# Small operations moved off VectorE in a six-layer decoder kernel: chains to GpSimd, mask and sums to TensorE, and a new walk

## The chip, the core and the metric

One core of a Trainium2 chip. The metric is the device time of one execution in microseconds, the median of several. The core has TensorE (PE, matrix products, its weight loads shown as PEld), VectorE (DVE), ScalarE (ACT), GpSimd (POOL) and SyncE (SP, which issues the DMAs). Each engine runs its own queue of instructions in order; they meet through semaphores.

## The reference

The input is x of 32 sequences, 128 tokens, 128 features, all float32, and a context of the same shape. Six blocks follow, and after each one `x = layernorm(x + block(x))`, without gain:

```
# L0_attn: a memory M (128x128) per sequence, two chunks of 64 tokens
y  = chunk @ M^T ; h = silu(y W1^T) W2^T + y                  # output of the chunk
km = mean(chunk / |chunk|) ; err = mean(h) - M km
M' = gate*(alpha*M + eta*err km^T) + (1-gate)*M ; M' *= min(30/(|M'|+1e-6), 1)
# L0_xattn: causal attention + x, norm (gain, bias), attention on the context + h, norm, relu(h W1 + b1) + h, norm, relu
# L0_ffn:   8 routed experts (4 with multipliers and a capacity) and a shared one
# L1_attn:  q,k,v = silu(conv4(x W)); T = I + tril(K K^T beta, -1) for chunks of 32; u = T^-1 v; w = T^-1 k; recurrence over
#           4 chunks; four causal filters of v (3, 7, 15, 31 taps); a router mixes the five paths; rms norm per head; Wo
# L1_xattn: attention on the context with biases
# L1_ffn:   top 2 of 4 experts; the third has two norms inside
```

## The kernel before

**Tiles.** The 32 sequences are 8 groups (`g` = 0 to 7) of 4 sequences, so that most tiles are 128 partitions by 512 elements (4 sequences of 128), of which one fills one of the 8 PSUM banks. Groups 0 to 3 and 6, 7 are loaded at the start; 6 and 7 run through the first two blocks early and are parked in DRAM; 4 and 5 are loaded when groups 0 and 1 leave. Each group runs through some 110 named steps; the first letter is the block (`a`, `x` with `c`, `f`, `b`, `y`, `g`).

**The order** of all steps is one text, `ORDER` (L38), written out by hand or by a planner that is not part of the kernel. `walk` reads it. Each engine's function (`sync`, `tensor`, `vector`, `scalar`, `gpsimd`) goes through the whole walk and issues what it has to do for a step. So the position in `ORDER` sets the place in every queue. `bank_table` deals out PSUM banks along the walk, each held until the step that `BANKS` names as the last.

**Steps that matter here.**

- *Norms.* `stats` on DVE (L1067) takes bn_stats and bn_aggr of each sequence, then makes the negated mean and the variance plus epsilon by two small instructions. POOL's `root` (L2101) takes the power -0.5 and multiplies the mean by it. ACT's `apply` (L1781) then normalizes in four instructions. There are 11 such norms per group (`STATS`), 88 in all.
- *The memory update.* DVE sums squares (`a_y`), makes silu from a tanh that ACT made (`a_s0`, `a_s1`), spreads the mean key (`a_km`), and makes the update's scalars by a chain of dependent instructions on 128x4 tiles (`a_dots` L1206, `a_c` L1239); POOL takes one square root in the chain.
- *Causal attention.* DVE adds the mask to the scores (`x_sc`, L1279), takes the row maximum and scales it; ACT makes the exponentials; DVE scales the product by the inverse sums and adds the residual (`x_pv`). In the attention on the context (`c_`), DVE multiplies the exponentials by the inverse sums (L1308) and TensorE adds the residual by a transposing product (`opened`, L492).
- *L1_attn.* TensorE makes the key norms and gates (`b_ss`, L790: eight products with 8 or 4 columns moving) and the query norms (`b_qn`, L803: four). DVE solves the triangular system by columns (`b_x`, 31 steps of two instructions, one multiplying and one subtracting).
- *L1_ffn.* `g_b0` (L961) makes the third expert's first product, `g_lg` (L966) the router's logits, four products each from the same input; DVE makes the weights (`g_wd`, L1691) and scales a transposed tile twice (`g_b2`, L1710). In L0_ffn, DVE splits the shares in three bfloat16 parts (`f_gl`, L1440).

`o.settle()` makes an engine wait for its own last linked instruction, so each dependent pair on one engine costs a semaphore's round.

Of the kernel before, what the change touches and what calls it, by code (L numbers as in the profile page):

```python
# [38 lines left out]
a_load/0 a_load/1 a_load/2 a_load/3 a_load/6 a_load/7 s_a a_y/0 a_s0/0 a_y/1 a_s0/1 c_v/0 a_ga/0 a_ga/1 c_v/1 a_km/0  # L39
a_km/1 a_err/0 a_err/1 a_dots/0 a_y/2 a_dots/1 a_c/0 a_y/3 a_s0/2 a_ga/2 s_x a_s1/0 a_c/1 c_v/2 a_km/2 a_out/0 a_s1/1  # L40
c_v/3 a_s0/3 s_f a_na/0 s_b1 s_b2 a_ga/3 x_tr/0 a_err/2 x_q/0 a_out/1 a_y/6 a_na/1 a_km/3 c_v/6 x_sc/0 a_dots/2 a_s0/6
x_ex/0 a_err/3 a_c/2 a_ga/6 x_tr/1 x_q/1 a_s1/2 c_v/7 a_dots/3 x_pT/0 x_sc/1 x_v/0 a_out/2 x_ex/1 a_km/6 x_pv/0 a_na/2
x_v/1 x_pT/1 a_y/7 x_tr/2 x_na/0 x_pv/1 x_q/2 a_s0/7 x_hF/0 x_v/2 c_q/0 s_y a_c/3 x_na/1 a_err/6 a_ga/7 a_s1/3 x_hF/1
a_km/7 c_sc/0 x_sc/2 c_ex/0 a_out/3 x_ex/2 c_q/1 a_dots/6 c_pT/0 a_err/7 c_pv/0 x_pT/2 a_na/3 a_c/6 c_sc/1 c_na/0
a_dots/7 x_pv/2 x_tr/3 c_hF/0 x_q/3 c_w1/0 a_s1/6 x_sc/3 c_ex/1 x_na/2 c_ft/0 s_g1 a_out/6 x_ex/3 x_v/3 c_fa/0 c_pT/1
x_hF/2 x_pT/3 s_g2 a_na/6 c_pv/1 c_nb/0 c_q/2 x_tr/6 s_g3 a_c/7 f_tr/0 c_na/1 x_pv/3 c_sc/2 a_s1/7 x_q/6 f_lg/0 x_na/3
f_mu/0 c_hF/1 f_hid.0-1/0 c_ex/2 a_out/7 x_v/6 c_w1/1 f_cnt/0 f_gl/0 x_hF/3 f_hid.2-4/0 c_ft/1 c_q/3 c_pT/2 a_na/7
x_sc/6 c_sc/3 f_gw/0 x_tr/7 f_hid.5/0 f_e.0-4/0 x_ex/6 c_fa/1 c_pv/2 x_q/7 f_e.5/0 c_ex/3 f_d.0-2/0 x_pT/6 x_sc/7
x_pv/6 c_nb/1 f_d.3-4/0 c_na/2 x_ex/7 f_d.5/0 c_pT/3 x_v/7 f_tr/1 x_na/6 f_out/0 f_na/0 c_pv/3 c_hF/2 c_na/3 x_pT/7
f_lg/1 f_mu/1 x_hF/6 c_w1/2 b_tr/0 c_hF/3 c_q/6 b_q/0 b_v/0 b_qs/0 b_q2/0 f_cnt/1 c_sc/6 f_hid.0/1 b_qn/0 b_vs/0  # L50
b_sh/0 b_k/0 b_vT/0 c_ft/2 b_ks/0 b_k2/0 f_hid.1-2/1 b_ez/0 x_pv/7 b_ss/0 c_ex/6 c_fa/2 f_hid.3-5/1 x_na/7 f_gl/1
c_w1/3 c_pT/6 b_fir.0-1/0 x_hF/7 c_nb/2 c_pv/6 c_q/7 f_gw/1 f_tr/2 c_sc/7 f_e.0-2/1 c_na/6 c_ft/3 c_ex/7 f_e.3-4/1
f_d.0/1 c_hF/6 f_e.5/1 f_d.1/1 c_w1/6 f_d.2/1 b_gg/0 f_d.3-4/1 c_ft/6 c_fa/3 c_fa/6 c_nb/3 c_nb/6 c_pT/7 c_park/6
f_d.5/1 f_out/1 f_na/1 b_fir.2-3/0 c_pv/7 c_na/7 b_tr/1 f_lg/2 f_mu/2 f_hid.0/2 b_v/1 b_q/1 b_kk/0 b_ag/0 b_sol/0
b_vs/1 b_sh/1 b_k/1 c_hF/7 b_qs/1 f_cnt/2 f_gl/2 b_q2/1 b_ks/1 b_k2/1 b_x.0-2/0 c_w1/7 f_hid.1/2 f_tr/3 b_x.3/0
f_hid.2/2 b_qn/1 b_x.4/0 f_gw/2 c_ft/7 b_x.5-9/0 f_hid.3-4/2 b_ez/1 f_e.0/2 b_x.10-11/0 c_fa/7 c_nb/7 f_e.1-2/2
c_park/7 b_vT/1 b_x.12-17/0 f_hid.5/2 b_fir.0/1 f_lg/3 b_ss/1 b_fir.1/1 f_d.0-2/2 f_e.3/2 f_mu/3 f_e.4/2 b_fir.2/1
f_hid.0-1/3 f_cnt/3 b_x.18/0 f_d.3/2 f_e.5/2 f_d.4-5/2 f_gl/3 f_out/2 f_hid.2-3/3 b_x.19/0 f_gw/3 f_hid.4/3
# [2224 lines left out]
```

## Time and profile before

| | us |
|---|---|
| three runs | 1147.06, 1147.66 (median), 1148.03 |
| the profiled execution | 1141.68 |
| its span, from first to last instruction | 1139.7 |
| PE busy | 1044.7 (92%) |
| DVE busy | 854.5 (75%) |
| ACT busy | 630.5 (55%) |
| POOL busy | 211.4 (19%) |

The profile's page lists busy time, the span in 40 slices, the DMA queues, the chain of work that ended last, and groups of instructions. The clock column is the TensorE clock that was granted, as a share of full speed. Busy time of PE is modelled, since products overlap in it.

### The profile page before, as it was taken

To read this page: it belongs to the slowest core of one execution; us is meant where nothing else is said; L and a number is where in the kernel's file an instruction comes from. 1 tells how busy PE (TensorE), PEld (TensorE's weight loads), DVE (VectorE), ACT (ScalarE), POOL (GpSimd) and SP (SyncE) were. 2 spreads that over 40 slices of the span, in tenths; PEclk is the share of its full clock that TensorE was granted. 3 is DMA by queue.
4 is the path that set the end of the run, shared out by engine and by line. 5 is a ranking of instruction groups with operands and counts; after the bars stand their busy time and mean duration, and the time that the engine had idled before them with its cause. 6 is when DMAs were issued, how large, how long until landed. Compare 5 with 4: busy or idle time off the path is not lost.

```text
span 1139.7 us, 21963 instructions
## 1 busy us (share of the span) xinstructions
PE 1044.7 (92%) x8036; PEld 714.2 (63%) x8036; DVE 854.5 (75%) x3375; ACT 630.5 (55%) x1341; POOL 211.4 (19%) x255
## 2 busy tenths in 40 slices
PE   5988889979998899999999967999998899999996
PEld 4767565545555577577777844464555567676775
DVE  3889998888869775777776468885988856787544
ACT  2466788674562124567777654645553134688662
POOL 0222223312121010222121120003131011331100
PEclk9899999988997589999999977999988699999998
DMA  9200001030243110001010000012242110000000
GB/s 336 89 1 1 1 1 47 10 74 11 56 91 69 20 30 2 18 2 38 2 28 10 18 20 10 1 46 57 68 93 56 38 29 10 10 11 1 1 10 28
DMA packets 71643, 41.24 MB, mean 36 GB/s; under 512 B 52208, under 2 KB 63856, under 8 KB 71280
## 3 DMA queue, kind: packets, MB, share of 16 engines
q1 hardware_dynamic: 71536, 39.84, 13.3%
q8 instruction: 64, 1.05, 0.4%
q14 instruction: 43, 0.35, 0.1%
HBM read 30.92 MB, written 8.91 MB: 35 GB/s over the span
## 4 chain that ended last, share of the span: by engine, by line
PE 67%; DVE 21%; ACT 6%; issue 2%; DMA 2%; POOL 1%; SPq 1%; POOLq 0%; ACTq 0%; DVEq 0%
PE psum L890 8%; PE psum L994 6%; PE psum L489 5%; PE psum L820 5%; PE psum L986 4%; PE psum L760 4%; PE psum L498 3%; DVE sol_t L1536 3%; DVE pool L1539 3%; ACT pool L1784 3%; PE psum L731 2%; PE psum L859 2%; PE psum L980 2%; PE psum L982 2%; PE psum L733 2%
## 5 line engine op out<-in xcount | busy, mean ns | idle before, releaser
L2105 POOL TENSOR_TENSOR small<-small,minus_half 128x4 f32<-128x4 f32 x88 | 91.8, 1044 | 485.9 <-DVE small L1079 485.6
L1770 ACT ACTIVATE pool<-psum 128x512 f32<-128x512 f32 x160 | 93.1, 597 | 116.9 <-PE psum L820 48.0
L1784 ACT ACTIVATE pool<-pool,small 128x128 f32<-128x128 f32 x256 | 105.3, 484 | 74.4 <-POOL small L2107 74.0
L489 PE MATMUL psum<-sb_const,pool 128*128 128x128 f32 x672 | 103.9, 291 | 25.5 <-ACT pool L1784 15.3
L489 PEld LDWEIGHTS psum<-sb_const,pool 128*128 128x128 f32 x672 | 82.1, 150 | 61.4 <-issue 23.7
L820 PE MATMUL psum<-pool,firw 128*32 128x512 f32 (+7 forms) x960 | 104.6, 584 | 1.6 <-POOL pool L2131 1.0
L890 PE MATMUL psum<-pool,sb_l1a 128*128 128x512 f32 x192 | 91.2, 629 | 0.0
L994 PEld LDWEIGHTS psum<-sb_l1f,pool 128*128 128x128 f32 x640 | 78.5, 194 | 11.6 <-issue 10.8
L994 PE MATMUL psum<-sb_l1f,pool 128*128 128x128 f32 x640 | 81.6, 278 | 0.0
L1338 DVE TENSOR_TENSOR pool<-pool,psum 128x512 f32<-128x512 f32 x80 | 52.2, 681 | 27.7 <-ACT pool L2018 14.7
L820 PEld LDWEIGHTS psum<-pool,firw 128*32 128x32 f32 x960 | 29.4, 112 | 64.4 <-issue 61.0
L1539 DVE TENSOR_TENSOR pool<-pool,sol_t 128x126 f32<-128x126 f32 (+22 forms) x248 | 63.3, 255 | 8.5
L1536 DVE TENSOR_TENSOR sol_t<-pool 128x126 f32<-128x126 f32 (+22 forms) x248 | 63.1, 254 | 7.5
L890 PEld LDWEIGHTS psum<-pool,sb_l1a 128*128 128x128 f32 x192 | 37.5, 201 | 43.2 <-issue 42.8
L1083 DVE SCALAR_TENSOR_TENSOR pool<-psum,small,pool 128x128 f32<-128x128 f32 x192 | 53.8, 342 | 14.2 <-PE psum L994 7.6
L1483 DVE SCALAR_TENSOR_TENSOR pool<-psum,taps,pool 128x508 f32<-128x508 f32 (+2 forms) x72 | 52.7, 741 | 6.8 <-ACT pool L1904 5.1
L1071 DVE BATCH_NORM_STATS2 small<-pool 128x6 f32<-128x128 f32 x256 | 55.8, 280 | 2.1
L859 PE MATMUL psum<-pool 32*32 32x32 f32 x1024 | 44.1, 205 | 12.4 <-DVE pool L1556 7.6
L731 PE MATMUL psum<-pool,sb_l0f 128*128 128x512 f32 x96 | 52.7, 632 | 1.6 <-DVE pool L1338 1.6
L859 PEld LDWEIGHTS psum<-pool 32*32 32x32 f32 x1024 | 40.4, 120 | 20.6 <-DVE pool L1556 10.0
L760 PEld LDWEIGHTS psum<-sb_l0f,pool 128*128 128x128 f32 x384 | 47.2, 200 | 8.6 <-issue 7.3
L1784 ACT ACTIVATE pool<-psum,small 128x128 f32<-128x128 f32 x96 | 36.0, 457 | 28.7 <-POOL small L2107 28.7
...
## 6 DMA issues: line engine op xcount, KB each, us to landing
...
```

Of the source, the lines that this page charges most:

```text
L489: m = e.transpose(f.ap[:, part(b)], src[:, part(b)], ident)
L731: e.matmul(f.ap, wt("l0f", "gate", k * P, P), slot(g, 1), start=True, stop=True).then_inc(f.filled, 1)
L760: m = e.matmul(f.ap[:, part(b)], slot(g, 2 + k)[:, part(b)], wt("l0f", "down", k * P, P), start=k == 0 and b == 0, stop=k == NHT - 1 and b ...
L820: m = e.matmul(b4(f.ap)[32 * c:32 * c + 32, :, 4 * kg:], firw[:, col, :], vsh[:, c, :, 0:P - 4 * kg], start=n == 0, stop=n == len(kgs) - 1)
L859: m = e.matmul(hd(f.ap)[r_, q, :], hd(slot(g, 13))[r_, q, :], src[r_, q, :], start=True, stop=True)
L890: m = e.matmul(f.ap, wt("l1a", "rw1", i * 256 + k * P, P), slot(g, src), start=i == 0, stop=i == 5)
L994: m = e.matmul(f.ap[:, part(b)], slot(g, 4 + k % 4)[:, part(b)], weight, start=k == first and b == 0, stop=k == last and b == GB - 1)
L1536: e.tensor_tensor(tmp, x[:, 0:nm, k:k + 1].to_broadcast([P, nm, ni]), a[:, k, k + 1:].unsqueeze(1).to_broadcast([P, nm, ni]), ALU.mult).th ...
L1539: m = e.tensor_tensor(x[:, 0:nm, k + 1:], x[:, 0:nm, k + 1:], tmp, ALU.subtract)
L1770: e.activation(slot(g, i), f.ap, ACT.Copy).then_inc(f.emptied, 1)
L1784: m = e.activation(dst[:, part(b)], src[:, part(b)], ACT.Identity, bias=v["nm"][:, b:b + 1], scale=v["r"][:, b:b + 1])
L2105: e.tensor_tensor(r, r, half[:, 0:GB], ALU.pow).then_inc(*mark("inverse_std", n_var[step, 0, g]))
```

## The change

What each part does:

1. **GpSimd makes more small chains.** `stats` ends with bn_aggr; `root` now also makes the negated mean and the raised variance. All of `a_dots` but the copy from PSUM (now ACT's), and the scalars of `a_c`, run on POOL, as 22 instructions in 13 dependent stages and a last pair. The split in thirds (`f_gl`) and the expert weights (`g_wd`) run on POOL too.
2. **ACT takes over** silu (its own function in the place of tanh and a DVE instruction) in `a_s0` and `a_s1`, the sums of squares in `a_y` (four instructions with an accumulated output in the place of one), the scaling of the probabilities in `x_ex` and `c_ex` (four instructions each), and `g_b2`. The score scale is folded into the queries with its sign turned, so that DVE takes a minimum and scales nothing.
3. **TensorE** adds the causal mask by a bfloat16 product of the identity with the mask, and the residual in `x_pv` by four transposing products. `a_err` is three products in the place of four. `a_c` reads the mean key through a broadcast, so the spread copy goes. `b_ss` is three products of 512 columns with 32 columns of weights each, written to partitions 0 to 31, 32 to 63 and 64 to 95 of one bank; ACT copies them out and `b_qn` transposes them. `g_lg`'s products are four more columns of `g_b0`'s, whose output is now in two banks.
4. **The solve** `b_x` has 62 half steps in the walk in the place of 31 steps; the instructions are the same.
5. **`ORDER`** is another walk of the same steps. The scores' bank in `x_sc` is held until the exponentials are made, that of `x_pv` until `x_na`.

The diff, cut to its core:

```diff
-        def stats(step, g, src, eps):
+        def stats(step, g, src):
...
             for b in range(GB):
                 m = e.bn_aggr(v["mv"][:, b, :], v["st"][:, b, :])
-            m.then_inc(*o.link())
-            o.settle()
-            e.tensor_scalar(v["nm"], v["mv"][:, :, 0], -1.0, None, ALU.mult)
-            e.tensor_scalar(v["r"], v["mv"][:, :, 1], eps, None, ALU.add).then_inc(sem("variance"), 1)
+            m.then_inc(sem("variance"), 1)
@@ gpsimd: root
             o.wait_ge(sem("variance"), n_var[step, 0, g])
+            e.tensor_scalar(nm, mv[:, :, 0], -1.0, None, ALU.mult)
+            e.tensor_scalar(r, mv[:, :, 1], eps, None, ALU.add).then_inc(*mark("variance_raised", n_var[step, 0, g]))
+            settle()
             e.tensor_tensor(r, r, half[:, 0:GB], ALU.pow).then_inc(*mark("inverse_std", n_var[step, 0, g]))
@@ gpsimd: a_dots (DVE's a_dots and the scalars of a_c go)
+            step(e.tensor_scalar(gate, gate, 0.5, 0.5, ALU.mult, ALU.add), 1)
+            e.tensor_tensor(c1, ea[:, GB:], gate, ALU.mult)
+            step(e.tensor_tensor(c2, gate, ea[:, 0:GB], ALU.mult), 2)
...
+            f = fill("a_dots", g)
+            o.wait_ge(f.emptied, f.n)
+            e.tensor_tensor(qq, qq, dots[:, 0, :], ALU.mult)
+            step(e.tensor_tensor(gate, dots[:, 1, :], dots[:, 2, :], ALU.mult), 6)
...
+            step(e.tensor_tensor(nn, nn, inv_half[:, 0:GB], ALU.pow), 10)
+            step(e.tensor_scalar(nn, nn, 1e-6, None, ALU.add), 11)
+            step(e.tensor_tensor(nn, nn, minus_one[:, :], ALU.pow), 12)
+            step(e.tensor_scalar(nn, nn, 30.0, 1.0, ALU.mult, ALU.min), 13)
@@ tensor: x_sc
-            for b in range(GB):
-                m = e.matmul(f.ap[:, part(b)], slot(g, 2)[:, part(b)], slot(g, 1)[:, part(b)], start=True, stop=True)
+            e.matmul(b4(f.ap), identb[:, :], rep_b(maskb[:, :]), start=True, stop=False)
+            for b in range(GB):
+                m = e.matmul(f.ap[:, part(b)], slot(g, 2)[:, part(b)], slot(g, 1)[:, part(b)], start=False, stop=b == GB - 1)
@@ vector: x_sc, x_ex, x_pv
-            e.tensor_tensor(b4(slot(g, 4)), b4(f.ap), rep_b(cmask), ALU.add).then_inc(f.emptied, 1)
-            got(f)
-            e.tensor_reduce(v["mx"], b4(slot(g, 4)), AX, ALU.max).then_inc(*o.link())
-            o.settle()
-            e.tensor_scalar(v["mx"], v["mx"], -float(P) ** -0.5, None, ALU.mult).then_inc(sem("x_max"), 1)
+            e.tensor_reduce(v["mx"], b4(f.ap), AX, ALU.min).then_inc(sem("x_max"), 1)
...
-            add_scaled(f, slot(g, 4), slot(g, 0), small[g]["sums"])
-            got(f)
-            stats("x_pv", g, slot(g, 4), 1e-3)
+            stats("x_pv", g, full("x_pv", g).ap)
@@ scalar: x_ex (c_ex alike)
+            softened(f, g, slot(g, 4), f.ap, "x").then_inc(f.emptied, 1)
+            o.wait_ge(f.emptied, f.n)
+            o.wait_ge(sem("x_inverse"), nth[g])
+            for b in range(GB):
+                m = e.activation(slot(g, 4)[:, part(b)], slot(g, 4)[:, part(b)], ACT.Copy, scale=small[g]["sums"][:, b:b + 1])
@@ tensor: b_ss, b_qn
-            for b in range(GB):
-                e.matmul(pn[:, b, 4:12], slot(g, 1)[:, part(b)], wt("l1a", "wb_id"), start=True, stop=True)
-                m = e.matmul(pn[:, b, 0:4], slot(g, 14)[:, part(b)], heads, start=True, stop=True)
+            for i, src in enumerate((14, 1, 13)):
+                c_ = slice(32 * i, 32 * i + 32)
+                m = e.matmul(f.ap[c_, :], sides[:, c_], slot(g, src), start=True, stop=True)
...
-                m = e.matmul(f.ap[:, b * 4:b * 4 + 4], slot(g, 13)[:, part(b)], heads, start=True, stop=True)
+                m = e.transpose(f.ap[:, 96 * b:96 * b + 96], slot(g, 12)[0:96, part(b)], ident[0:96, 0:96])
@@ tensor: g_b0 (g_lg's products go)
-            by_token(begin("g_b0", g), slot(g, 1), wce[:, :])
+            for i, label in enumerate(("low", "high")):
+                f = begin("g_b0", g, label)
+                for b in range(2):
+                    m = e.matmul(f.ap[:, 132 * b:132 * b + 132], slot(g, 1)[:, part(2 * i + b)], wce[:, :], start=True, stop=True)
@@ ORDER, a place of each
-... a_err/0 a_err/1 a_dots/0 a_y/2 a_dots/1 a_c/0 a_y/3 a_s0/2 a_ga/2 s_x a_s1/0 a_c/1 ...
+... a_err/0 a_dots/0 a_s0/1 a_ga/1 a_km/1 a_y/2 a_c/0 a_y/3 a_err/1 c_v/1 a_s0/2 a_ga/2 c_v/2 a_s0/3 a_dots/1 ...
-... b_x.20-21/0 f_na/2 b_x.22-23/0 f_hid.5/3 f_e.0-1/3 b_tr/2 ... b_x.24-25/0 b_gg/1 ...
+... f_d.0/3 f_e.5/3 b_x.19-24/0 f_d.1/3 b_sol/1 f_d.2-3/3 b_x.25-61/0 b_xo/0 ...
```

## Rows read from the trace of the kernel before

**Rows 1.** The page, part 1: busy time, share of the span, instructions.

```profile
PE 1044.7 (92%) x8036; PEld 714.2 (63%) x8036; DVE 854.5 (75%) x3375; ACT 630.5 (55%) x1341; POOL 211.4 (19%) x255
```

**Rows 2.** Stretches: length, busy us and count of each engine, clock, DMA share, GB/s.

```profile
28.50:285.00 256.50, 223.70 (x1367) 153.78 (x1366) 226.39 (x1024) 166.89 (x407) 65.51 (x84) 0.95 0.09 26
285.00:342.00 57.00, 55.89 (x570) 31.54 (x572) 42.53 (x135) 31.61 (x76) 10.73 (x13) 0.97 0.33 74
342.00:399.00 57.00, 48.57 (x618) 31.20 (x611) 47.16 (x162) 13.06 (x30) 4.07 (x2) 0.67 0.22 44
399.00:655.50 256.50, 252.94 (x1884) 186.85 (x1883) 175.84 (x667) 157.68 (x312) 48.07 (x56) 0.99 0.06 17
655.50:712.50 57.00, 40.10 (x148) 26.32 (x147) 41.65 (x220) 28.42 (x64) 9.82 (x16) 0.70 0.05 15
712.50:855.00 142.50, 140.34 (x1075) 80.50 (x1073) 116.06 (x415) 76.84 (x158) 26.60 (x27) 0.96 0.23 53
855.00:912.00 57.00, 48.49 (x646) 31.99 (x639) 50.51 (x174) 13.42 (x31) 2.90 (x1) 0.76 0.24 48
912.00:1111.50 199.50, 199.46 (x1554) 144.40 (x1553) 130.49 (x476) 126.77 (x234) 38.73 (x44) 1.00 0.04 10
```

**Rows 3.** Waits, longest in total: engine and line, releaser: us, times, longest.

```profile
ACT pool L1784 <- POOL small L2107: 102.7, 45, 8.1
```

**Rows 4.** Groups of DVE instructions by form: count, busy us, mean ns, idle before.

```profile
L1308 DVE TENSOR_TENSOR pool<-pool,small 128x512 f32<-128x512 f32 x8 | 5.5, 692 | 0.3
L1162 DVE TENSOR_REDUCE small<-pool 64x4 f32<-64x512 f32 x8 | 5.4, 676 | 7.9 <-ACT pool L1798 7.9
L1083 DVE SCALAR_TENSOR_TENSOR pool<-psum,small,pool 128x128 f32<-128x128 f32 x192 | 53.8, 342 | 14.2 <-PE psum L994 7.6 <-PE psum L953 3.5 <-PE psum L498 1.3
L1712 DVE TENSOR_SCALAR pool<-psum,sb_l1f 128x512 f32<-128x512 f32 x8 | 6.4, 802 | 0.6 <-PE psum L489 0.6
L1078 DVE TENSOR_SCALAR small<-small 128x4 f32<-128x4 f32 x88 | 15.1, 171 | 3.0
L1237 DVE TENSOR_SCALAR small<-small 128x4 f32<-128x4 f32 x8 | 1.4, 169 | 0.3
```

**Rows 5.** Groups of POOL instructions by form.

```profile
L2105 POOL TENSOR_TENSOR small<-small,minus_half 128x4 f32<-128x4 f32 x88 | 91.8, 1044 | 485.9 <-DVE small L1079 485.6
L2107 POOL TENSOR_TENSOR small<-small 128x4 f32<-128x4 f32 x88 | 19.7, 224 | 6.9
L2154 POOL TENSOR_TENSOR pool<-pool 128x512 f32<-128x512 f32 x8 | 10.1, 1268 | 160.4 <-DVE pool L1604 160.4
```

**Rows 6.** Groups of ACT instructions by form.

```profile
L1784 ACT ACTIVATE pool<-pool,small 128x128 f32<-128x128 f32 x256 | 105.3, 484 | 74.4 <-POOL small L2107 74.0
L1776 ACT ACT_TABLE_LOAD x10 | 12.8, 1283 | 0.2
```

**Rows 7.** The chain that ended last, pieces: start us, us, what.

```profile
118.98 0.66 PE psum L489 x4
205.06 0.75 PE psum L754 x3
325.11 6.26 PE psum L820 x64
484.54 0.86 PE psum L980 x2
555.39 0.89 PE psum L971 x8
```

**Rows 8.** Timeline of DVE, then of POOL, near 217 us.

```profile
216.81 0.69 DVE L1327 SCALAR_TENSOR_TENSOR pool<-pool 128x512 f32<-128x512 f32 x1
...
216.99 0.56 POOL L2107 TENSOR_TENSOR small<-small 128x4 f32<-128x4 f32 x1
```

**Rows 9.** The chain again, the same work at two clocks.

```profile
388.29 8.02 PE psum L890 x12
...
398.35 5.35 PE psum L890 x12
```

More of the change, by code:

```diff
@@ L38 @@
 ORDER = """
[L39 to L58, printed above, removed]
@@ L79 @@
-g_e3/1 g_h.2/2 g_tr/3 g_e0/1 g_b2/2 g_b7/1 g_e2/1 g_h.0-1/3 g_b0/3 g_wT/2 a_na/4 a_load/5 a_y/5 x_tr/4 g_lg/3 g_b3.0/2
-x_q/4 g_st/1 c_v/5 g_b1/3 x_sc/4 g_wd/3 x_v/4 x_ex/4 g_d.0/2 g_eb/2 g_h.3/2 g_b3.1/2 x_pT/4 a_s0/5 g_d.1-2/2 x_pv/4
-x_na/4 g_b4/2 a_ga/5 g_h.2-3/3 x_hF/4 g_h.4-6/2 a_km/5 c_q/4 g_na/0 g_wT/3 a_err/5 c_sc/4 c_ex/4 g_d.3/2 g_e0/2
-g_h.7/2 g_d.4-5/2 g_h.8/2 g_e1/2 g_b2/3 g_d.0/3 g_out/0 g_b5/2 a_dots/5 g_h.4/3 c_pT/4 g_d.1-2/3 g_b3.0/3 g_eb/3 a_c/5
-g_h.5-6/3 g_b3.1/3 a_s1/5 g_na/1 g_d.3-4/3 c_pv/4 c_na/4 a_out/5 g_e0/3 g_d.5/3 g_e1/3 g_h.7/3 a_na/5 g_d.6/2 g_b4/3
@@ new lines @@
+a_y/4 b_nF/3 y_sc/2 y_ex/2 a_s0/4 y_v/3 a_ga/4 g_b1/1 g_d.0-1/1 b_wo/3 y_pT/2 g_e3/0 a_km/4 g_wT/1 g_b2/1 g_st/0
+y_pv/2 y_k/3 g_h.4-5/1 g_eb/1 b_na/3 y_na/2 g_d.2-3/1 g_h.6/1 g_d.4/1 a_err/4 g_h.7/1 g_e0/1 a_dots/4 g_b3.0/1 g_d.5/1
+g_e1/1 g_tr/2 a_c/4 g_h.0/2 g_b3.1/1 g_b4/1 g_h.1/2 a_s1/4 c_v/4 y_tr/3 a_out/4 g_b5/1 g_b0/2 g_d.6/1 y_q/3 g_b6/1
+g_h.8-9/1 a_na/4 g_b7/1 g_e2/1 g_b1/2 g_d.0/2 g_lg/2 y_sc/3 g_h.2-3/2 x_tr/4 g_d.7/1 g_wd/2 x_v/4 y_ex/3 x_q/4 g_b2/2
+g_d.1/2 y_pT/3 x_sc/4 x_ex/4 g_wT/2 g_d.8/1 g_b3.0/2 y_pv/3 x_pT/4 a_load/5 g_b3.1/2 y_na/3 x_pv/4 g_b4/2 x_na/4
@@ new lines @@
+g_d.2/2 g_d.9/1 g_h.4-6/2 x_hF/4 g_tr/3 g_d.3/2 g_eb/2 c_q/4 g_h.7/2 c_sc/4 g_e3/1 g_st/1 a_y/5 g_na/0 g_d.4-5/2
+g_h.8/2 g_e1/2 a_s0/5 a_ga/5 c_v/5 g_b0/3 g_h.0/3 c_ex/4 a_km/5 g_lg/3 g_wd/3 g_e0/2 g_h.9/2 g_b5/2 g_d.6-7/2 g_d.0/3
+c_pT/4 a_err/5 g_h.1/3 g_out/0 g_b6/2 g_wT/3 c_pv/4 g_b1/3 g_h.2/3 c_na/4 g_d.8/2 g_d.1/3 g_b2/3 a_dots/5 g_h.3/3
+c_hF/4 g_b7/2 g_e2/2 g_d.2/3 c_w1/4 g_eb/3 g_d.3/3 c_ft/4 g_b3.0/3 a_c/5 g_b3.1/3 a_s1/5 f_load/6 a_out/5 g_na/1
+c_fa/4 g_d.9/2 g_h.4-6/3 a_na/5 g_b4/3 g_h.7/3 g_d.4-5/3 c_nb/4 g_h.8/3 x_tr/5 f_tr/4 g_e3/2 g_st/2 x_q/5 g_b5/3
@@ L1858, in c_ex @@
             softened(f, g, slot(g, 4), f.ap, "c").then_inc(f.emptied, 1)
+            o.wait_ge(f.emptied, f.n)
+            o.wait_ge(sem("c_inverse"), nth[g])
+            for b in range(GB):
+                m = e.activation(slot(g, 4)[:, part(b)], slot(g, 4)[:, part(b)], ACT.Copy, scale=small[g]["sums"][:, b:b + 1])
+            m.then_inc(sem("c_probs"), 1)
         def c_pT(g, k):
@@ L1938, in b_gg, with b_ss @@
         def b_gg(g, k):
-            f, z = fill("b_ss", g), small[g]["z"]
+            f, z = fill("b_qn", g), small[g]["z"]
             o.wait_ge(f.emptied, f.n)
             e.activation(z, z, ACT.Tanh, scale=0.5).then_inc(sem("z_tanh"), 1)
+        def b_ss(g, k):
+            f = full("b_ss", g)
+            e.activation(slot(g, 12)[0:96, :], f.ap[0:96, :], ACT.Copy).then_inc(f.emptied, 1)
         def b_vT(g, k):
@@ L2138, in b_ss @@
                 *mark("key_norm", g + 1))
-        def b_qn(g, k):
-            f, rq = fill("b_qn", g), small[g]["rq"]
+            f, rq = fill("b_qn", g), v["rq"]
             settle()
```

495 lines of the change are left out of this document (250 added, 245 removed), and 1 row of the table BANKS.

## The prediction

> **What bounds the kernel now.** I read the busy times first [rows 1]. PE is busy for 1044.7 of 1139.7 us, so 95 us of idle PE is all that a better order alone can win at this clock. What stands there as busy is also stretched where the clock is low. Then I cut the span into stretches [rows 2]. From 399 to 655.5 us and from 712.5 to 855 us and from 912 to 1111.5 us PE is busy to 98.6%, 98.5% and 100%: there only work taken from PE counts. From 28.5 to 285 us PE is idle for 32.8 us while DVE is busy for 226.4 of 256.5 (88%). That is the largest gap, and DVE has the most work in it after PE; the waits name the chain from a norm's scalars on POOL to ACT as well: 102.7 us in 45 waits, most of them beside busy PE [rows 3]. In 342 to 399 and 855 to 912 us DVE is busy for 47.2 and 50.5 of 57 us, with the solve, and PE idles 8.4 and 8.5 us at a mean clock of 0.67 and 0.76. In 655.5 to 712.5 us PE idles 16.9 us, the clock is 0.70. The ends of the span hold another 22 us that no part of the change touches.
>
> **PE's work, part by part.** At full clock four products with few columns moving take 0.89 us, four transposes 0.66, one product of 512 columns 0.86 [rows 7]; so 0.22, 0.165 and 0.86 each.
> - `b_ss` and `b_qn` before: 12 products of 0.22 = 2.7 us per group. After: three products with 32 columns of weights. The filters are of this kind, and 64 records of them, 32 products, take 6.26 us [rows 7]: four side by side in 0.78. I take 0.86 for the three, and 0.66 for the four transposes, so 1.5 in all: -1.2 us per group, -9.6 in all. If the three ran one after the other they would cost 2.6 us, and the part +0.5 per group.
> - `g_lg`: four products go, -0.89 us, and `g_b0` has 4 columns more in each, between nothing and 4/128 of 0.89: -0.9 per group, -7.2.
> - `a_err`: one product less, -0.22 per group, -1.8.
> - The mask: one bfloat16 product of 512 columns. Three records of that type take 0.75 us [rows 7], so +0.25 per group, +2.0.
> - The residual in `x_pv`: four transposing products, +0.66 at most; they come in turns with others, so I take 0.6, +4.8.
> The sum is -11.8 us. Of it the logits (-7.2) lie wholly in stretches where PE is full. Of the eight groups' `b_ss`, six lie from 285 us on in nearly full stretches.
>
> **DVE's work.** A small instruction takes 0.17 us [rows 4]. Per group go 60 of them: 22 of the norms, 21 of the update's scalars, 3 scalings of a maximum, 8 of the thirds, 6 of the expert weights: 10.2 us. Two instructions of 512 elements with two inputs (mask, probabilities) go at 0.69, the sum of squares at 0.68, four of `x_pv` at 0.342, two in `g_b2` at 0.80 [rows 4]: 5.0. Three of 256 or 512 simple elements (two of silu, the spread key) have no row here; they lie between 0.17 and 0.69, and I take 0.42, 1.3 in all. `g_b0` in two halves costs about +0.5. That is -16 us per group, -128 us in all, of 854.5. In the stretch to 285 us, where six groups pass the first two blocks, it is some 10.3 us each and 5 of L0_ffn: about -67, so DVE falls from 226 to 160 us there. It is no longer what holds PE.
>
> **What ACT takes.** Eight scalings of 128x128 per group at 0.41 (105.3 over 256) [rows 6]: +3.3. `g_b2`, two of 512 elements: between four and zero of those 0.41, I take +1.4. The split squares, four of 128 for one of 512 and their sums: between 0 and +1.9, I take 1.0. The copy of `b_ss` +0.6, the scalars' copy +0.25. With small gains elsewhere +6.3 per group, +50. Tables: with one table each for the exponential, silu and gelu, and tanh in every one, counting along the walk of before gives 84 loads, and the trace has 84, at 1.28 us [rows 6]. Along the new walk the same count gives 87, six of them for the new silu: +3.9 us. ACT comes to some 684 us, and in the stretch to 285 us to 203, under PE's 225. So none of it is on the path by its amount. A reciprocal on DVE now stands between the exponentials and the product, with ACT waiting; there are 16 such waits, each between 0.2 us and a full 0.7 us instruction that DVE has in hand. Behind the waiting scalings stand ACT's copies for other groups.
>
> **What POOL takes.** An instruction on 4 elements takes 0.22 us, a power 1.04, a sum of 512 elements 1.27 [rows 5], and 0.08 us pass between two dependent ones (6.9 over 88). A norm gets two more, side by side: about +0.3 us until ready, against the 0.3 that DVE saves. So no norm gets shorter or longer by more than the wait in DVE's queue. The update is 22 instructions with two powers: 20 x 0.22 + 2 x 1.04 + 14 x 0.08 = 7.6 us for a group. On DVE the same chain was 21 x 0.17 plus one power = 4.6 us, but in a queue that was full. The thirds are 6 instructions of 0.3 to 0.4, the weights 6 with a power: about 2.2 us each. POOL goes from 211 to about 320 us, 29% of the span.
>
> A two-input instruction on DVE holds up one of POOL: at 216.99 us a POOL multiplication that takes 0.20 to 0.22 alone lasts 0.56 us, and ends just after the DVE instruction with both inputs in SBUF that runs from 216.81 to 217.50 [rows 8]. The Trainium skill, page "SBUF — State Buffer", section "Who interferes with whom", has this as a lock: a DVE instruction with two SBUF inputs contends with a GpSimd one that reads SBUF, and the one that issued second waits for the first to end. The trace agrees. By that rule the 440 or so small instructions new to POOL each risk up to 0.69 us, 300 us in sum at the worst; it would only be paid where nothing else covers it. By the trace the mean of 88 such multiplications is 0.224 us against 0.20 free, so I take +0.02 each and put the rest in the slower rival.
>
> **The half steps.** Of the 496 half steps in the new walk, 463 are followed on DVE by the next half of the same group, so they run as before. The 33 splits can fill 0.03 to 0.3 us each. I take -1.
>
> **The sum**, against the profiled execution's 1141.68 us:
> - 28.5 to 285: PE's work becomes 223.7 + 6 x 0.85 (mask, residual) - 6 x 0.22 - 2 x 1.2 = 225. With DVE free I give PE 94% of the stretch, between the 87% now and the 98.5% of the full stretches: 239.5, so -17. The ends are -1 (share kept) and -28.
> - 285 to 342: two groups' norms of keys, -2.4.
> - 399 to 655.5 and 912 to 1111.5: the logits -7.2, one product of `a_err` -0.4, and two late groups' mask and residual +1.7: -5.9 together.
> - 712.5 to 855: four groups, -4.8.
> - 655.5 to 712.5: DVE loses about 15 of 41.7 us while PE idles 16.9; I take -5, between 0 and -15.
> - 342 to 399 and 855 to 912: the solves are not shorter (47 us of DVE for three groups), only what comes before them is; -6 for both, between +4 and -16.
> - half steps -1.
> That is -42.1, so 1099.6 for such an execution. The profiled one stood 5.98 us below the median of the three, so the median after is **1105.6 us**.
>
> **The rivals.**
> - *The front is held by dependence, not by DVE's load.* ACT's waits for POOL [rows 3] speak for it, and that each group's chain gets no shorter. DVE at 88% speaks against. Then the 17, 5 and 6 us don't come: 1105.6 + 28 = 1134.
> - *The clock comes back too.* The mean clock of 0.93 is 160 us at the lower level, 1.2 in the place of 2.4 GHz. It is lowest in the three stretches of 57 us in which PE idles, mean 0.71, where PE is busy for 137 us, so some 80 of these at half clock. The same 12 records take 8.02 us there and 5.35 later [rows 9], so a third of the 80, 28 us, is to be had if PE has no gaps: 1078. Against it: the solves stay.
> - *The products aren't side by side*: 1.72 us more per group, 1119.
> - *Slower: POOL's queue.* Every norm of every group passes one queue, and now stands behind chains of 7.6 us that themselves wait for PE and ACT in their middle (about 9 us in the queue). In the new walk the norm of `a_out/0` stands right behind the update of group 1, `c_pv/0` near that of 6, `x_pv/2` behind that of 7. If each of the eight chains holds up a norm whose group is what PE waits for, that is 8 x 7.2 = 58 us: 1164. It decides from 5.3 us per chain on, where it has eaten the 42. For it: 485.9 us of POOL's idle time was waiting for DVE [rows 5], so it was always ready before. Against: it is 71% idle, and four groups are in flight.
>
> **How the numbers follow.** Chances: the forecast 0.49, with its own range 1086 to 1121; dependence 0.14; the clock 0.15; products in turn 0.04; POOL's queue 0.14; 0.04 that the terms cancel within 0.2%, which is about what a measurement of this kernel tells from no change. Faster 0.82, same 0.04, slower 0.14. The range is 1070 to 1142: it takes in the clock and the dependence, and leaves out POOL's queue and the tails.
>
> **What would show it.** In the profile after: POOL 300 to 340 us, DVE 715 to 740, ACT 670 to 700 with 87 table loads. PE 1025 to 1040 if the clock stays. Three products of `b_ss` within 1 us. PE's share in the stretch after 28.5 us above 0.92. DVE's idle time there grows. Wrong would be: PE waiting on the norms' scalars more than now (POOL's queue), ACT over 90% in the front, or a walk whose stretches at low clock grow, since I gave the new order nothing in either direction.

## The result, and the profile after

The kernel after takes 1127.76 us (median of 4 runs, 1126.39 to 1129.52), the kernel before 1147.36 on the same chip; the ratio is 0.9836, 95% interval 0.9811 to 0.9861. It is faster, by 19 us (19.6 between the medians), under half of the 42 that the prediction worked out. The time lies within the wide range of 1070 to 1142, which took in two rivals, and outside the forecast's own, 1086 to 1121. Below, "against after" means the difference of two such ratios, 0.001 being 1.15 us; its own uncertainty is 4 to 8 us, said where it matters.

The page, part 1, of the kernel after (as [rows 1]):

```profile
PE 1024.5 (91%) x7884; PEld 690.0 (61%) x7884; DVE 748.5 (67%) x2822; ACT 670.7 (60%) x1497; POOL 324.9 (29%) x696
```

Its stretches, with the bounds and columns of [rows 2]. The bounds are the same times and not the same steps, since the order is another:

```profile
28.50:285.00 256.50, 228.59 (x1461) 156.43 (x1462) 180.05 (x761) 198.42 (x513) 113.69 (x287) 0.98 0.09 27
285.00:342.00 57.00, 49.26 (x461) 26.74 (x463) 46.83 (x158) 26.51 (x66) 8.31 (x12) 0.76 0.38 84
342.00:399.00 57.00, 54.93 (x794) 37.92 (x787) 49.19 (x166) 16.84 (x36) 5.96 (x2) 0.85 0.21 39
399.00:655.50 256.50, 247.85 (x1707) 179.52 (x1705) 150.14 (x574) 172.15 (x359) 84.22 (x178) 0.97 0.06 17
655.50:712.50 57.00, 42.01 (x190) 26.97 (x191) 33.71 (x143) 29.00 (x61) 11.87 (x30) 0.88 0.03 10
712.50:855.00 142.50, 135.36 (x1199) 69.47 (x1198) 113.58 (x398) 73.29 (x155) 34.13 (x50) 0.96 0.27 62
855.00:912.00 57.00, 49.02 (x568) 35.11 (x566) 46.98 (x152) 14.95 (x33) 1.26 (x1) 0.68 0.18 34
912.00:1111.50 199.50, 198.17 (x1436) 142.98 (x1435) 115.93 (x419) 126.71 (x239) 56.04 (x103) 0.99 0.03 9
```

The span fell from 1139.7 to 1125.0 us. PE's busy time fell by 20.2 us, and its idle time rose from 95.0 to 100.5. So nothing was won from idle PE, where the prediction had most of its gain, although DVE has 106 us less. In the first stretch DVE fell from 226 to 180 us, and PE's idle time only from 32.8 to 27.9. In the three stretches that were full in [rows 2] (285 to 342, 399 to 655.5, 712.5 to 855) idle PE rose from 6.8 to 23.5 us (57 - 49.26, 256.5 - 247.85, 142.5 - 135.36): as much as was taken from PE there, and more, stands as gaps.

The chain that ended last, its first line, of before and then of after:

```profile
PE 67%; DVE 21%; ACT 6%; issue 2%; DMA 2%; POOL 1%; SPq 1%; POOLq 0%; ACTq 0%; DVEq 0%
```

```profile
PE 56%; DVE 18%; ACT 16%; POOL 4%; issue 3%; DMA 2%; SPq 1%; POOLq 0%; ACTq 0%; DVEq 0%
```

The chain left PE and DVE for ACT and POOL: 10% and 3% of the span more stand on these. What POOL does in the front (the stretches up to about 300 us) is in its timeline of the kernel after (start us, us, instruction; in brackets what it waited for before):

```profile
97.19 0.19 POOL L2083 TENSOR_SCALAR small<-small 128x4 f32<-128x4 f32 x1
...
100.73 1.04 POOL L2101 TENSOR_TENSOR small<-small,plus_half 128x4 f32<-128x4 f32 x1
...
104.48 0.20 POOL L2108 TENSOR_TENSOR small<-small 128x4 f32<-128x4 f32 x1
105.65 0.23 POOL L2052 TENSOR_SCALAR small<-small 128x4 f32<-128x4 f32 x1 [0.97 <-DVE small L1079]
...
107.26 0.20 POOL L2057 TENSOR_TENSOR small<-small 128x4 f32<-128x4 f32 x1
107.85 0.23 POOL L2052 TENSOR_SCALAR small<-small 128x4 f32<-128x4 f32 x1 [0.39 <-DVE small L1079]
...
110.04 0.23 POOL L2052 TENSOR_SCALAR small<-small 128x4 f32<-128x4 f32 x1
```

One group's scalars of the update run from 97.19 to 104.68, 7.5 us, and then three norms follow at 1.8 to 2.4 us each. An engine that is 29% busy over the span has hardly a gap here. Still the update held up none of these norms: the first two began only when DVE had delivered (the waits of 0.97 and 0.39 us in brackets), and the third 0.45 us after DVE's last instruction for it, behind the second. From there the chain of waits goes on into ACT (the same kernel, start us, us, what):

```profile
110.64 1.15 POOL small L2055
111.79 0.07 issue
111.86 0.61 POOL small L2057
112.47 0.02 issue
112.50 1.65 ACT pool L1697 x4
114.15 1.39 ACT pool L1689 x8
```

How far the first blocks are is seen better from a step than from a fixed time. In the order of both kernels `f_out/3` is the last of the steps `f_out` of groups 0 to 3, and groups 6 and 7 have passed their first two blocks by then. Its norm begins on POOL at 311.87 us before and at 308.74 after (in the walk's order it is found by counting POOL's norms):

```profile
311.87 1.01 POOL L2105 TENSOR_TENSOR small<-small,minus_half 128x4 f32<-128x4 f32 x1 [3.60 <-DVE small L1079]
```

```profile
308.74 0.23 POOL L2052 TENSOR_SCALAR small<-small 128x4 f32<-128x4 f32 x1 [11.01 <-DVE small L1079]
```

So some 3 us of the gain are there by then (one profiled execution of each, and executions of one kernel differ by some us), where the forecast had 17 for the front and 2.4 for the norms of the keys. PE had been busy for as long, 266.1 and 266.7 us, and its idle time until then fell by 3.7 us, from 45.8 to 42.1. After has 82 records more by then, only a part of them the change's own, so it was a little further on than the 3 us say (the stretch from 0 to this time, columns of [rows 2], before and then after):

```profile
0.00:311.87 311.87, 266.11 (x1640) 180.65 (x1640) 259.97 (x1154) 188.13 (x456) 69.65 (x98) 0.95 0.18 57
```

```profile
0.00:308.74 308.74, 266.66 (x1722) 178.91 (x1726) 208.01 (x867) 217.78 (x566) 120.06 (x315) 0.98 0.20 61
```

### The profile page after: what moved, and what is told of

It reads as the page before. It is cut to its first block, busy times and chain, and to the rows that moved or that the text cites. A ratio compares the mean times of both kernels' runs of the same rounds, so it can differ in the third digit from the quotient of the medians.

```text
span 1125.0 us, 21764 instructions
## 1 busy us (share of the span) xinstructions
PE 1024.5 (91%) x7884; PEld 690.0 (61%) x7884; DVE 748.5 (67%) x2822; ACT 670.7 (60%) x1497; POOL 324.9 (29%) x696
## 4 chain that ended last, share of the span: by engine, by line
PE 56%; DVE 18%; ACT 16%; POOL 4%; issue 3%; DMA 2%; SPq 1%; POOLq 0%; ACTq 0%; DVEq 0%
PE psum L898 7%; PE psum L998 5%; PE psum L828 5%; PE psum L493 4%; ACT pool L1697 4%; PE psum L990 3%; DVE pool L1465 3%; DVE sol_t L1470 3%; PE psum L502 2%; PE psum L986 2%; PE psum L984 2%; PE psum L867 2%; POOL small L2055 2%; ACT pool L1689 2%; ACT pool L1683 2%
## 5 line engine op out<-in xcount | busy, mean ns | idle before, releaser
L1683 ACT ACTIVATE pool<-psum 128x512 f32<-128x512 f32 x144 | 83.2, 595 | 97.2 <-PE psum L828 36.2
L1697 ACT ACTIVATE pool<-pool,small 128x128 f32<-128x128 f32 x224 | 91.9, 483 | 77.8 <-POOL small L2057 77.8
L493 PE MATMUL psum<-sb_const,pool 128*128 128x128 f32 x672 | 106.3, 295 | 33.9 <-ACT pool L1697 14.8
L2052 POOL TENSOR_SCALAR small<-small 128x4 f32<-128x4 f32 x88 | 22.5, 256 | 346.7 <-DVE small L1079 344.8
L828 PE MATMUL psum<-pool,firw 128*32 128x512 f32 (+7 forms) x960 | 101.3, 574 | 0.3 <-POOL pool L2128 0.3
L1697 ACT ACTIVATE pool<-psum,small 128x128 f32<-128x128 f32 x128 | 47.9, 461 | 22.2 <-POOL small L2057 22.2
L1084 DVE SCALAR_TENSOR_TENSOR pool<-psum,small,pool 128x128 f32<-128x128 f32 x160 | 44.6, 342 | 23.2 <-PE psum L998 17.1
L1075 DVE BATCH_NORM_STATS2 small<-pool 128x6 f32<-128x128 f32 x224 | 48.8, 281 | 2.4
L740 PE MATMUL psum<-pool,sb_l0f 128*128 128x512 f32 x96 | 49.1, 593 | 1.1 <-DVE pool L1414 1.1
L738 PE MATMUL psum<-pool,sb_l0f 128*128 128x512 f32 x96 | 49.9, 602 | 0.0
```

The source lines that it names most:

```text
L493: m = e.transpose(f.ap[:, part(b)], src[:, part(b)], ident)
L828: m = e.matmul(b4(f.ap)[32 * c:32 * c + 32, :, 4 * kg:], firw[:, col, :], vsh[:, c, :, 0:P - 4 * kg], start=n == 0, stop=n == len(kgs) - 1)
L1683: e.activation(slot(g, i), f.ap, ACT.Copy).then_inc(f.emptied, 1)
L1697: m = e.activation(dst[:, part(b)], src[:, part(b)], ACT.Identity, bias=v["nm"][:, b:b + 1], scale=v["r"][:, b:b + 1])
```

## The experiments

**Is it the order or the edits, and does the solve take the gain back?** Four kernels. `old_code_new_walk` is before with after's ORDER:

```
-ORDER (before)          +ORDER (after), b_x as half steps; nothing else
```

> The code of before with the order of the kernel after (and its solve cut in half steps, without which that order can't be written). No other edit is in it. If the gain of 19.6 us comes from the edits of the operations, this one is at 1140 to 1150 us, no faster than before. If the new order makes the gain and the moved operations bring little, it is at 1128 to 1134 us. If the order only fits the new operations (it sets DVE's steps closer than the old DVE work allows), it is slower than before: 1155 us or more.

Measured: 1176.69 us, ratio 1.0251 (1.0190 to 1.0312), 29 us slower than before. The new order alone is no gain; it only fits the operations it comes with. All the new operations in the old order were not tried; two parts of them were (`before_moved`, below).

`before_no_solve` and `after_no_solve` keep only the copy in `b_x`:

```
-            e.tensor_tensor(tmp, x[...], a[...], ALU.mult)
-            e.tensor_tensor(x[...], x[...], tmp, ALU.subtract)
```

> The kernel before, with the steps of the triangular solve left out (only the copy of the unit rows stands, in both layers' halves), so DVE has some 130 us less of work in the stretches 200 to 400 and 700 to 870 us. It is read against the kernel after with the same steps left out. If the solve is the stage that takes back what the front gains, the two differ by more than the whole kernels do: by 28 to 40 us. If not, they differ by the same 20 us or less. Its own time: 1060 to 1110 us.

> The kernel after, with the steps of the triangular solve left out as in the kernel before without it. If the solve takes back what the front gains: 28 to 40 us faster than the kernel before without solve. If the gains are simply smaller than forecast: 15 to 22 us faster than it.

Measured: 1126.89 us (0.9835, 0.9796 to 0.9873) and 1108.90 (0.9670, 0.9626 to 0.9714). They are 18 to 19 us apart, as the whole kernels are: the solve takes nothing back. That theory falls. And 121 us less of DVE (854.5 to 733.5) bring before 19 us, 0.16 us for one; I put this down to the queues, which stay in order and hold the rest in place, but no run isolates it.

**Is it ACT's amount?** `no_scaling` leaves out what `x_ex` and `c_ex` gave to ACT; `scale_and_sq_dve` moves it, and the squares' sums, to DVE:

```
-            for b in range(GB):
-                m = e.activation(slot4[b], slot4[b], ACT.Copy, scale=sums[b])
+            (no_scaling: nothing)   (scale_and_sq_dve, on DVE: slot4 * rep(sums), one instruction)
```

> The kernel after, with the scaling of the probabilities (four ACT operations of 389 ns in each x_ex and c_ex, 16 steps, 25 us in all) left out, so ACT has 25 us less and nobody else has more. If ACT has become the bound of the stretch from 85 to 200 us, where it is busy 93% of the time, this kernel is 5 to 15 us faster than the one after (1113 to 1123 us). If chains of dependent operations hold the front, not an engine's amount, it gains only where the scaling stands in a chain: 1 to 4 us (1124 to 1127 us). If the solve takes back what the front gains, the front's milestones come 5 to 10 us earlier and the end moves by 1 or 2.

> The kernel after, with two of the things that went to ACT back on DVE: the scaling of the probabilities (16 steps: one DVE multiply of 0.80 us for four ACT scalings of 0.39 us) and the sums of the squares (8 steps: one ACT square and one DVE sum for four ACT squares with their sums). ACT has some 35 us less, DVE some 17 us more. If ACT's amount holds the stretch from 85 to 200 us, where DVE is busy only 61 and 82% of it, this is faster than the kernel after by 6 to 12 us (1116 to 1122 us). If chains hold the front, it is within 3 us of 1127.8. If DVE's order is as tight as before, it is slower: 1130 us or more.

Measured: `no_scaling` 1120.52 (0.9766, 0.9726 to 0.9806), 8 us faster than after; `scale_and_sq_dve` 1129.84 (0.9858, 0.9825 to 0.9891), 2.5 us slower than after, within the uncertainty of 5. ACT has 23 us less in the second (647.8) and nothing is won. But DVE has 16 us more in it (764.3), and by the price of DVE's time in `dve_filler` (below) these could have eaten a gain: that ACT's load does not hold the front is not shown. Between 85 and 200 us ACT is busy for 106.6 of 115 us (93%) in the kernel after, which I had named as a sign of being wrong. What `no_scaling` gains may as well be its shorter chain, four scalings less in each of 16 steps; the two runs don't tell these apart.

**Part by part, undone.** Update's scalars, norms' small operations, silu back on DVE:

```
dots_dve:   a_dots, first part of a_c as before; GpSimd: the root alone
stats_dve:  DVE: nm = -mean, r = var + eps; GpSimd: pow, product
silu_dve:   ACT: tanh; DVE: (t + 1) * u
```

> The kernel after, with the scalars of the update (a_dots and the first part of a_c) made by DVE as in the kernel before, GpSimd making only the root, and ACT's copy of the products gone. If the longer chain on GpSimd (two powers of 1.04 us and some 17 operations of 0.20 to 0.26 us in each of 8 groups) costs the front time, this is 2 to 6 us faster than the kernel after. If it frees DVE at no price, this is slower by the DVE time it puts back (8 groups of 3.5 us, of which the front feels the six groups before 200 us): 4 to 12 us slower, 1132 to 1140 us.

> The kernel after, with the negated mean and the variance plus eps of all norms made by DVE as before (two DVE operations of 0.1 to 0.17 us and a wait between) and GpSimd making only the root and the product. If GpSimd's two more operations in the chain of each norm (0.2 to 0.26 us each) cost more than DVE's, this is 1 to 4 us faster than the kernel after; if DVE's time is what counts, 3 to 8 us slower; if neither, within 2 us of 1127.8.

> The kernel after, with the first memory layer's silu made as before, by ACT's tanh and a DVE operation of 0.44 us from PSUM, 16 of these. ACT's busy time stays as it is, DVE gets 7 us more, and each such step has one hand-over more before PE can go on. If the front is held by chains, this costs 3 to 8 us (1131 to 1136 us); if ACT's amount holds it, 0 to 2 us.

Measured: `dots_dve` 1136.39 (0.9903, 0.9868 to 0.9938), 7.7 us slower than after; `silu_dve` 1133.56 (0.9887, 0.9855 to 0.9918), 5.9 slower; `stats_dve` 1123.45 (0.9802, 0.9770 to 0.9835), 3.9 faster, within its uncertainty. In the new order the update on POOL and the direct silu pay, each just beyond what can be told; that the norms' operations on POOL bring anything can't be told.

**Amount or length of the chain.** One kernel adds a power to POOL's link in each norm, one adds four sums to DVE (each of them waited for), one takes one operation out of the link, one shortens two:

```
root_longer: +  e.tensor_tensor(idle_pow, inv_half, inv_half, ALU.pow)   between root and product
dve_filler:  +  4 x e.tensor_reduce(idle_sum, unit_rows)                 at the head of DVE's a_c
split_stats: nm = -mean on DVE, behind the semaphore of bn_aggr; r = var + eps stays on GpSimd
best1:       split_stats, and the scaling of the probabilities on DVE
```

> The kernel after, with one more power of 1.04 us, on a tile that nobody reads, between the root and the product in GpSimd's chain of each of the 88 norms. GpSimd is busy 29% of the span, so its amount can't matter; its link in every chain of dependent steps gets some 1.1 us longer. If chains hold the fronts, where PE is idle, the kernel is 10 to 25 us slower (the 48 norms of the two fronts at 0.2 to 0.5 us each): 1138 to 1153 us. If engines' amounts hold it, the price is under 3 us.

> The kernel after, with four sums over a constant (128x512, 0.68 us each, into a tile that nobody reads) at the head of DVE's a_c in each of 8 groups, before its wait for GpSimd: 22 us more of DVE, as much as dots_dve gave back to it, but with the chain on GpSimd kept. Where DVE would otherwise stand waiting for the chain, it costs nothing. If the 8.6 us of dots_dve came from DVE's amount, this is 1133 to 1138 us. If they came from how the chain runs, this is within 2 us of 1127.8.

> The kernel after, with the negated mean alone back on DVE, behind the semaphore that lets GpSimd begin, so it stands beside the root. GpSimd's chain of each norm loses one operation of some 0.2 us, and no operation comes in its place in the chain; DVE gets 88 operations of 0.1 us and a wait on its own last write. stats_dve, which moved two operations, was 4 us faster than the kernel after. If the chain's length makes the time: 1121 to 1125 us, no slower than stats_dve. If what counts is how long DVE is held: 1127 us or more.

> The kernel after with split_stats's edit and with the scaling of the probabilities by one DVE multiply of 0.8 us for four ACT operations of 1.28 to 1.56 us (the sums of the squares stay with ACT). Both shorten a chain: if the chains' length makes the time, it is at 1116 to 1122 us. scale_and_sq_dve, which moved the squares too, gained nothing; if the scaling's part of that was a loss, this is 1125 us or more.

Measured: `root_longer` 1175.91 (1.0279, 1.0219 to 1.0339), 51 us slower than after; `dve_filler` 1158.06 (1.0123, 1.0074 to 1.0173), 33 slower, for 22 us of DVE; `split_stats` 1127.67 (0.9845, 0.9789 to 0.9900) and `best1` 1129.29 (0.9881, 0.9842 to 0.9921), no gain. Both cost far more than expected, and neither of the two ways to shorten a chain gave anything. Amount and length are not told apart by this: the power is 91 us more of POOL as well as a longer link, and the sums stand ahead of `a_c`, so that they delay the update as well as they load DVE. `best1` also gives DVE 26 us more (774.6). Their pages, `root_longer` first:

```profile
PE 1042.7 (89%) x7884; PEld 698.5 (59%) x7884; DVE 750.6 (64%) x2822; ACT 671.1 (57%) x1497; POOL 416.3 (35%) x784
```

```profile
PE 1047.5 (91%) x7884; PEld 706.2 (61%) x7884; DVE 771.0 (67%) x2854; ACT 672.5 (58%) x1497; POOL 324.6 (28%) x696
```

POOL has 91 us more in the first and the span is 49 us longer; DVE 22 more in the second, and the span is 32 longer. PE's work is the same in all three, yet its busy time is 18 and 23 us more than after's 1024.5: both wait more than after and have a lower clock (0.924 and 0.917 over the span, after 0.937). The first stretch of `dve_filler`, with the columns of [rows 2], has a granted clock of 0.89 where after has 0.98, 1.0 being the level of 2.4 GHz and 0.5 that of 1.2:

```profile
28.50:285.00 256.50, 225.66 (x1327) 161.84 (x1329) 175.63 (x704) 185.51 (x485) 108.47 (x276) 0.89 0.09 26
```

**The same two loads on before, the load moved late, and the link emptied.**

```
before_filler, before_root_longer: the two edits above, in the kernel before
late_filler:      the four sums at the head of DVE's b_wo in place of a_c
stats_left_out:   r = pow(var), nm = mean * r on GpSimd; no sign, no eps
```

> The kernel before, with dve_filler's four sums (22 us of DVE in all) at the same place, at the head of a_c, where DVE waits for GpSimd's root. In the kernel after they cost 30 us (1158 against 1128). If DVE was the bound of the front of before and is so no longer, the price here is higher: 30 to 40 us (1177 to 1188). If the price is that of a delay put into the order at this place, whichever engine is the bound, it is the same 22 to 30 us. If DVE's waits in before hide it, under 10 us.

> The kernel before, with root_longer's added power in GpSimd's chain of each norm. In the kernel after it costs 48 us for 97 us of GpSimd. If after hangs more on the chains than before did (DVE relieved, chains longer), before pays less: 20 to 38 us (1167 to 1185). If the chains held before just as much, the price is the same 45 to 50 us.

> The kernel after, with the four sums at the head of DVE's b_wo in each of 8 groups instead of a_c: again 22 us of DVE, but in the stretches 430 to 560 and 960 to 1080 us, where PE is busy 98 to 100%. If DVE's time costs something only where PE is idle, this is within 4 us of 1127.8. If the order is so tight that a delay of DVE costs time anywhere, it is slower by 10 us or more.

> The kernel after, without the two small operations of each norm on GpSimd (the negated mean, the variance plus eps), made by nobody, so that each chain is a power and a product: the computation leaves out the sign and the eps. GpSimd has 40 us less. By root_longer's rate (48 us of time for 97 us of chain) this is 15 to 22 us faster than the kernel after: 1106 to 1113 us, and what these two operations cost is about what their leaving DVE brought. If shortening a chain gives less than lengthening it costs, since another wait is next: 2 to 8 us faster.

Measured: `before_filler` 1169.69 (1.0200, 1.0161 to 1.0238), 23 us slower than before; `before_root_longer` 1188.69 (1.0349, 1.0282 to 1.0416), 40 us slower; `late_filler` 1143.26 (0.9987, 0.9963 to 1.0011), 17 us slower than after; `stats_left_out` 1115.57 (0.9719, 0.9687 to 0.9750), 13 us faster than after. The prices per microsecond: DVE at `a_c` 1.0 in before and 1.5 in after; POOL's link 0.4 and 0.55; DVE at `b_wo`, where PE is 98% busy, still 0.8. After hangs no less on either engine than before did. `late_filler` shows that "PE is full" does not mean that the others have slack; as I read it, the busy PE consumes what the next queue delivers just in time.

**The disputed step by itself, in the order of before.** `before_moved` moves the norms' two operations and the update's scalars to GpSimd and nothing else. `before_left_out` has nobody make them:

```
-   DVE: nm, r of each norm; the chain of a_dots; seven operations of a_c
+   before_moved: GpSimd's root and a_dots, DVE's a_c, ACT's copy of dots as in after
+   before_left_out: pow(var), mean * r; nn = ea * dots, c1 = ea * nn, c2 = nn * err
```

> The kernel before, its order untouched, with two parts of the change alone: GpSimd makes the negated mean and the variance plus eps of each norm and the scalars of the update (DVE 44 us less, GpSimd 90 us more, ACT 8 small copies more). If DVE's relief is worth what the forecast took it for, this is 8 to 15 us faster than before (1132 to 1139 us). If the longer chains take as much as the relief gives, it is within 4 us of 1147. If an order made for DVE's chain pays for GpSimd's and gets nothing back: 1152 to 1165 us.

> The kernel before, its order untouched, with the same small operations left out of DVE and made by nobody (the negated mean, the eps, and the update's scalars but for two products): the relief of DVE (40 us) and shorter chains as well, with no price anywhere. It is the most that this part could bring in this order. If the forecast's rate held, it is 10 to 17 us faster (1130 to 1137 us); if a relief in this order brings as much as a load costs (1.0 us for 1 us by before_filler), 25 to 40 us faster (1107 to 1122 us). Its distance to before_moved is the price of the chains on GpSimd.

Measured: `before_moved` 1173.34 (1.0243, 1.0201 to 1.0284), 28 us slower than before; `before_left_out` 1129.16 (0.9855, 0.9802 to 0.9908), 17 us faster. Their pages, in this order:

```profile
PE 1054.8 (90%) x8036; PEld 720.4 (62%) x8036; DVE 812.7 (69%) x3031; ACT 631.8 (54%) x1349; POOL 300.2 (26%) x600
```

```profile
PE 1038.3 (92%) x8036; PEld 708.7 (63%) x8036; DVE 814.8 (72%) x3063; ACT 629.8 (56%) x1341; POOL 211.0 (19%) x255
```

DVE is the same in both, 40 us under [rows 1]; they differ by POOL's 89 us (and ACT's 8 copies), and by 44 us of time, 0.5 us for one, as `root_longer` has it. So the relief of 40 us on DVE is worth 17 at most, since `before_left_out` shortens the chains as well, and making the operations on GpSimd costs 44 against nobody making them. The longest waits of ACT, and then of DVE, for POOL in `before_moved` (times, longest at the end):

```profile
ACT pool L1739 <- POOL small L2070: 128.0, 50, 9.3
```

```profile
DVE pool L1211 <- POOL small L2121: 21.2, 6, 6.4
```

The first was 102.7 us in 45 waits in [rows 3], and is 91.8 in 40 in `before_left_out`; the second is DVE at `a_c`, waiting for scalars that it used to make itself.

Part of it is a queue. At 118.53 us of `before_moved` a norm begins on POOL right behind the last instruction of an update, 6.45 us after DVE had finished for it at 112.08, and ACT waits 7.28 us for that norm (POOL's, DVE's and ACT's timeline):

```profile
118.25 0.20 POOL L2121 TENSOR_TENSOR small<-small 128x4 f32<-128x4 f32 x1
118.53 0.46 POOL L2065 TENSOR_SCALAR small<-small 128x4 f32<-128x4 f32 x1
```

```profile
111.70 0.38 DVE L1075 BATCH_NORM_AGGREGATE small<-small 128x2 f32<-128x6 f32 x4
```

```profile
120.62 1.50 ACT L1739 ACTIVATE pool<-psum,small 128x128 f32<-128x128 f32 x4 [7.28 <-POOL small L2070]
```

Two more norms stand like this, at 128.18 and 592.55 us (5.1 and 3.1 us), 15 us for the three. In the kernel after only one norm begins right behind an update (41.58 us), and it loses 0.2 us: there the order has the updates where no norm is waiting.

Where the two effects arise is seen at `f_out/3` again, now with one order in both and in before. Its norm begins at 335.24 us in `before_moved` and at 296.82 in `before_left_out` (311.87 before), so 23 us of the loss and 15 of the gain are there by then. The stretches up to it, in this order:

```profile
0.00:335.24 335.24, 276.48 (x1636) 188.44 (x1640) 236.67 (x960) 188.79 (x462) 119.65 (x292) 0.91 0.17 53
```

```profile
0.00:296.82 296.82, 257.67 (x1636) 176.12 (x1640) 238.19 (x984) 187.60 (x456) 69.35 (x98) 0.98 0.19 60
```

The products are the same ones (1636 and 1640 records; before 266.11 us at 0.95). The loss of 23 us is 13 of idle PE and 10 of the same products at a lower clock; the gain of 15 is 7 of idle PE and 8 of products at a higher one, by one execution of each.

## Why the prediction was wrong

**The step that failed** is the one of the stretch from 28.5 to 285: "With DVE free I give PE 94% of the stretch ... so -17", and with it the claim on ACT and POOL that "none of it is on the path by its amount", by which their additions cost nothing. PE has 89% of it (228.59 of 256.5), from 87%, and at `f_out/3` some 3 us are won and not 19. Shown in its place: DVE's relief does bring something (at most 17 us for 40, in `before_left_out`, 15 of them in the front), and making the operations on POOL costs more than that where the order is the old one (44 us between `before_left_out` and `before_moved`). In after's order the net of all edits is positive, -48 us between `old_code_new_walk` and after (uncertain by 8), and of it 6 to 8 each are the silu and the update. How much of the rest is the order fitting the operations, and how much the other edits, stays open. I had given the order nothing in either direction; alone it costs 29 us, and the edits in it bring the 48.

**Full stretches.** "There only work taken from PE counts", I wrote of 399 to 655.5. PE's busy time there fell by 5.1 us (252.94 to 247.85), and by 1.3 in 912 to 1111.5; the forecast for the two was 5.9. But the 5.1 stand as idle time in the same stretch: other work did not fill it. `late_filler` fits this, where 22 us of DVE at `b_wo` cost 17; that it is the reason is not shown. In 655.5 to 712.5 idle PE fell by 1.9 us where I took 5. In the two stretches with the solve (-6) it fell by 6.9, 6.4 of it in 342 to 399; but from 285 to 342, just before, it rose by 6.6, which may be the same gap at another time, and its clock fell from 0.97 to 0.76, a stretch at low clock that was not there before.

**PE's work** was right. The products of `b_ss` and `b_qn` fell from 21.7 to 13.3 us (-8.4 for -9.6), the logits' own products were 6.4 and `g_b0` grew by 1.3 (-5.1 for -7.2), `a_err` -3.0 for -1.8, the mask +1.7 for +2.0, the residual +4.4 for +4.8: -10.4 for -11.8, each product counted from the end of the one before. The other 9.8 us of the 20.2 are the net of the same products in less time (`f_hid` -5.0, `f_d` -3.6, `b_fir` -3.0) and in more (`b_q`, `b_k` and `b_v` +6.6), with the clock of the whole at 0.937 from 0.930. The three products of `b_ss` take 1.1 us together, where one alone is 0.86 [rows 7]: side by side.

**The engines' sums** were right or nearly: DVE 748.5 (715 to 740 forecast), ACT 670.7 (670 to 700) with 88 table loads for 87, POOL 324.9 (300 to 340), the update's chain 7.5 us for 7.6. One term was mis-sized: DVE lost 106 us and not 128, and has 180 us in the first stretch where I had 160. In `before_moved` 344 instructions fewer are 41.8 us less, so a small one is worth 0.12 us and not the 0.17 that it lasts by itself; for 60 per group in 8 groups that is 23 us, about the 22 missing (an estimate). That is not the step that failed: even right sums don't say who waits for whom.

**The rivals.** "Dependence holds the front" (1134, chance 0.14) is the nearest to what the runs show, though it spoke of PE's front alone. "POOL's queue" (1164, 0.14) had up to 58 us for norms held up behind the updates. In the old order such norms exist, three of them with 15 us in sum (`before_moved`); the rest of its 44 us is the longer links and DVE's own wait for the scalars, which the runs don't part. In the new order the queue costs next to nothing. I held against it that POOL is 71% idle, and that is no argument for a link in a chain: `root_longer` is 51 us slower with POOL 65% idle. ACT's waits for the norms stayed the same in sum, 100.0 us in 36 waits after 102.7 in 45 [rows 3], though the longest grew from 8.1 to 14.4 us; in that one (up to 310.77 us) POOL itself was waiting for DVE, at the norm of `f_out/3`. The Trainium skill's page "Perfetto Trace Analysis", section "Optimizing GPSIMD Operations", says to prefer other engines where possible, GpSimd being slower in general; here one operation of 4 elements takes 0.20 to 0.26 us on it where DVE takes 0.17 [rows 4], and the norms' operations are a part where the runs don't contradict the rule (`stats_dve` is not slower), while the update's are one where they do (`dots_dve` is). The lock between DVE and GpSimd, [rows 8], had no visible price in the mean: L2057 takes 227 ns, 224 before [rows 5].

**Clock.** I had a rival in which it comes back as PE's gaps close (28 us). PE's gaps did not close as a whole and the clock rose only from 0.930 to 0.937, though it is 0.98 after 0.95 up to `f_out/3`. The runs in the old order show the effect both ways, 10 us of the loss and 8 of the gain in the front. In the new order `root_longer` has 31 us more of idle PE and 18 us more of busy time for the same products, `dve_filler` 9 and 23. A link that delays PE is paid a second time, and not in proportion to the idle time.
